# A recurrent memory layer gated by an int-quantised FFN: three elementwise jobs change engine, and the attention jobs move to other slots

## The reference

```
xn = layernorm(x)
# memory: for each of the 2048 steps, M0 is 128 x 128
q, k, v = xn @ Wq.T, xn @ Wk.T, xn @ Wv.T          # 512 -> 128 each
r_t = q_t @ M.T ;  M = 0.99 * M + v_t.T @ k_t / 4
s = (r @ Wo.T) * sigmoid(gate)                     # 128 -> 512
# FFN on layernorm(xn): weights int, one scale for 128 rows of a column
y = silu(h @ dequant(fc1_q) + b1)                  # 512 -> 2048
z = y @ dequant(fc2_q) + b2                        # 2048 -> 512
out = x + s * silu(xn + 0.5 * z)
```

## Time and profile before

| | |
|---|---|
| Time, median of 3 executions | 1356.86 us (1355.76 to 1358.03) |
| The profiled execution's own time | 1356.22 us |
| Its span, first to last instruction | 1354.4 us |
| Share of the span busy: PE, DVE, ACT, POOL | 91%, 80%, 76%, 45% |
| Mean granted TensorE clock | 0.973 |
| DMA engines' mean traffic | 48 GB/s |

### The profile page before, as it was taken

One profiled execution on the slowest core, in us unless ns is written; L12 is line 12 of the kernel. 1 busy time (PEld: TensorE's weight loads), 2 busy tenths in 40 slices (PEclk: granted clock), 3 DMA queues, 4 the chain that ended last, 5 costly groups with the idle time before them and its releaser, 6 DMA issues.

```text
span 1354.4 us, 18593 instructions
## 1 busy us (share of the span) xinstructions
PE 1227.3 (91%) x5888; PEld 588.1 (43%) x5888; DVE 1076.9 (80%) x1829; ACT 1032.3 (76%) x1805; POOL 608.7 (45%) x638
## 2 busy tenths in 40 slices
PE   0359999999999999999999999999999999999993
...
DMA packets 41620, 65.68 MB, mean 48 GB/s; under 512 B 11696, under 2 KB 11952, under 8 KB 41008
## 3 DMA queue, kind: packets, MB, share of 16 engines
...
q10 hardware_dynamic: 288, 0.08, 0.0%
...
## 4 chain that ended last, share of the span: by engine, by line
PE 61%; ACT 22%; issue 10%; DVE 3%; POOL 2%; DMA 1%; SPq 0%; ACTq 0%; POOLq 0%; DVEq 0%
PE blk L447 22%; PE blk L465 20%; PE side L408 9%; ACT blk L550 8%; PE side L432 4%; ACT y_full L557 4%; ACT h_full L512 3%; PE side L424 2%; PE side L417 2%; ACT g_hi L506 2%; ACT y_split L565 2%; ACT z_rows L573 1%; PE side L426 1%; PE side L425 1%; DMA xt<-in_x 1%
## 5 line engine op out<-in xcount | busy, mean ns | idle before, releaser
L680 DVE TENSOR_TENSOR blk<-blk,ratio_rows 128x512 f32<-128x512 f32 x960 | 647.4, 692 | 182.7 <-PE blk L465 180.3
L550 ACT ACTIVATE blk<-blk,ratio 128x512 f32<-128x512 f32 x768 | 519.8, 683 | 181.5 <-PE blk L447 176.1
L447 PE MATMUL blk<-h_split,q_sb 128*128 128x512 f16 x2048 | 614.4, 382 | 43.8 <-ACT q_sb L591 29.0
L465 PE MATMUL blk<-w_sb,y_split 128*128 128x512 f16 x2048 | 609.4, 380 | 6.4 <-POOL w_sb L968 5.6
L465 PEld LDWEIGHTS blk<-w_sb,y_split 128*128 128x128 f16 x2048 | 199.6, 98 | 251.4 <-issue 6.9
L447 PEld LDWEIGHTS blk<-h_split,q_sb 128*128 128x128 f16 x2048 | 183.1, 98 | 289.4 <-ACT blk L550 80.2
L951 POOL TENSOR_TENSOR h_split<-h_full,h_split 128x512 f16<-128x512 f32 x64 | 81.7, 1276 | 478.5 <-DVE h_split L656 464.0
L557 ACT ACTIVATE y_full<-blk,par,last 128x512 f32<-128x512 f32 x256 | 204.6, 799 | 73.5 <-PE blk L447 72.5
L671 DVE SCALAR_TENSOR_TENSOR y_split<-y_full,up,y_split 128x512 f16<-128x512 f32 x256 | 222.5, 869 | 0.0
L565 ACT ACTIVATE y_split<-y_full,up 128x512 f16<-128x512 f32 x256 | 190.7, 745 | 0.0
L999 POOL TENSOR_TENSOR z_rows<-z_rows,s_rows 128x512 f32<-128x512 f32 x62 | 79.0, 1274 | 63.6 <-ACT z_rows L573 63.6
...
## 6 DMA issues: line engine op xcount, KB each, us to landing
...
x_again<-in_x SPq DMA_DIRECT2D x256, 64.0 KB, 1.9
out<-z_rows SPq DMA_DIRECT2D x256, 64.0 KB, 1.7
...
```

Of the source, the lines that this page charges most:

```text
L447: mm = pe.matmul(blk[J % 2][:], q1_sb[:, g, j // 4, w, j % 4 * P:(j % 4 + 1) * P], a[:, c % 2, g, :], start=(g == 0 and n == 0), stop=(g = ...
L465: mm = pe.matmul(blk2[i][:], y[:, J % Y_RING, rows], w2_sb[:, j, part, :], start=(j == 0 and n == 0), stop=(j == FB - 1 and n == len(terms ...
L550: act.activation(blk[J % 2][:], blk[J % 2][:], ACT.Copy, scale=ratio1[:, at:at + 1]).then_inc(blk_scaled, 1)
L680: dve.tensor_tensor(blk2[i][:], blk2[i][:], ratio2_rows[:, j, :], ALU.mult).then_inc(blk2_scaled, 1)
```

## The change

Three jobs change engine: `y_high` goes from ACT to DVE (where `y_low` follows it one slot later, at lag 2 and not 3), and `normalise` and `h_high` go from DVE to POOL. For chunk 0 both stay on DVE, as `first_normalise` and `first_h_high`. The side jobs of a tile stand at offsets 0, 4, 7, 10 and 13 from its start, where they stood at 0, 4, 6, 8 and 11. With tiles 12 slots apart, a tile's wo now comes one slot behind the next tile's qkv. The turns stand at 51, 54, 56 and 59, and their lags are equal for all four. The four PSUM tiles of fc2 become four slices of one tensor; each product still has a bank of its own.

```diff
-TILE_AT, JOB_AT = (1, 13, 25, 37), (0, 4, 6, 8, 11)
-TURN_AT = (49, 52, 55, 58)
-QKV_LAG, QKT_LAG, R_LAG, S_LAG, GHIGH_LAG, HFULL_LAG = 1, 1, 1, 1, 1, (2, 2, 2, 3)
+TILE_AT, JOB_AT = (1, 13, 25, 37), (0, 4, 7, 10, 13)
+TURN_AT = (51, 54, 56, 59)
+QKV_LAG, QKT_LAG, R_LAG, S_LAG, GHIGH_LAG, HFULL_LAG = 1, 1, 1, 1, 1, 2
...
-STATS_AT, MOMENTS_AT, NORMALISE_AT = (0, 1, 2, 3), (5, 6), (33, 34, 37, 40)
-MASK_LAG, MEM_LAG, SPLIT_LAG, YHIGH_LAG, YLOW_LAG = 1, 1, (3, 3, 3, 4), 1, 3
-HLOW_LAG = 5
+STATS_AT, MOMENTS_AT = (0, 1, 2, 3), (5, 6)
+MASK_LAG, MEM_LAG, GLOW_LAG, YHIGH_LAG, YLOW_LAG = 1, 1, 3, 1, 2
+HSPLIT_LAG = 3
+NORMALISE_AT = (36, 38, 40, 42)
...
         @block.scalar
-            def y_high(J):
...
-                act.activation(y_hi[:, J % Y_RING, :], y_full[:, J % 2, :], ACT.Copy, scale=up_y
-                               ).then_inc(y_hi_done, 1)
...
         @block.vector
+            def y_high(J):
+                dve.wait_ge(silu_done, J + 1)
+                wait(dve, blk2_done, NT * (J - Y_RING + 1))
+                dve.tensor_scalar(y_hi[:, J % Y_RING, :], y_full[:, J % 2, :], up_y, None, ALU.mult
+                                  ).then_inc(y_hi_done, 1)
...
         @block.gpsimd
+            def normalise(c, i):
+                if i == 0:
+                    pool.wait_ge(rows_done, c + 1)
+                    pool.wait_ge(turn_done, 4 * c)
+                pool.tensor_scalar(g_rows[:, i, :], xt[:, i, :], mv[:, c % 2, i, 0:1],
+                                   gs[:, c % 2, i:i + 1], ALU.subtract, ALU.mult).then_inc(g_done, 1)
+
+            def h_high(c, k):
+                pool.wait_ge(h_full_done, 4 * c + k + 1)
+                if k == 0 and c >= 2:
+                    pool.wait_ge(blk_done, FC1_COUNT[FB * (c - 1) - 1, KC - 1])
+                pool.tensor_copy(h_hi[:, c % 2, k, :], h_full[:, k % 2, :]).then_inc(h_hi_done, 1)
...
+                if at := job_behind(G, HSPLIT_LAG, "turn"):
+                    h_high(*at)
                     h_low(*at)
```

More of the change, by code:

```diff
@@ L224, in build @@
         blk = [ctx.enter_context(nc.psum_tensor(f"blk{n}", [P, T], F32)) for n in range(2)]
-        blk2 = [ctx.enter_context(nc.psum_tensor(f"blk2_{n}", [P, T], F32)) for n in range(KC)]
+        blk2 = ctx.enter_context(nc.psum_tensor("blk2", [P, NT, H], F32))
         side = [ctx.enter_context(nc.psum_tensor(f"side{n}", [P, T], F32)) for n in range(2)]
-        first_turn_bank = blk2
+        first_turn_bank = [blk2[:, k, :] for k in range(KC)]
         par_in, wq_in, wo_in, m_in, gate_in = (
@@ L464, in ffn2 @@
                 for n, (y, part) in enumerate(terms):
-                    mm = pe.matmul(blk2[i][:], y[:, J % Y_RING, rows], w2_sb[:, j, part, :],
+                    mm = pe.matmul(blk2[:, i, :], y[:, J % Y_RING, rows], w2_sb[:, j, part, :],
                                    start=(j == 0 and n == 0), stop=(j == FB - 1 and n == len(terms) - 1),
@@ L610, in _ @@
                         silu(at[0])
-                if (at := fc1_step(G - YHIGH_LAG) if G >= YHIGH_LAG else None) and at[1] == KC - 1:
-                    y_high(at[0])
                 if at := job_behind(G, QKV_LAG, "qkv"):
@@ L622, in _ @@
                     g_high(*at, side[JOB_BANK[G - GHIGH_LAG]])
-                for k in range(KC):
-                    at = job_behind(G, HFULL_LAG[k], "turn")
-                    if at and at[1] == k:
-                        h_whole(*at, side[JOB_BANK[G - HFULL_LAG[k]]])
+                if at := job_behind(G, HFULL_LAG, "turn"):
+                    h_whole(*at, side[JOB_BANK[G - HFULL_LAG]])
                 if at := finishing(G, GATE_AT):
@@ L638, in moments, with first_h_high, first_normalise @@
                 dve.bn_aggr(mv[:, c % 2, i, :], stat6[:, i, :]).then_inc(mv_done, 1)
-            def normalise(c, i):
+            def first_h_high(k):
+                dve.tensor_copy(h_hi[:, 0, k, :], h_full[:, k % 2, :]).then_inc(first_h_hi_done, 1)
+            def first_normalise(i):
                 if i == 0:
-                    dve.wait_ge(rows_done, c + 1)
-                    wait(dve, turn_done, 4 * c)
-                dve.tensor_scalar(g_rows[:, i, :], xt[:, i, :], mv[:, c % 2, i, 0:1],
-                                  gs[:, c % 2, i:i + 1], ALU.subtract, ALU.mult).then_inc(g_done, 1)
+                    dve.wait_ge(rows_done, 1)
+                dve.tensor_scalar(g_rows[:, i, :], xt[:, i, :], mv[:, 0, i, 0:1],
+                                  gs[:, 0, i:i + 1], ALU.subtract, ALU.mult).then_inc(first_g_done, 1)
             def g_low(c, k, bank):
@@ L650, in g_low @@
                 dve.tensor_tensor(g_lo[:, k, :], bank[:], g_hi[:, k, :], ALU.subtract).then_inc(g_lo_done, 1)
-            def h_high(c, k):
-                if k == 0 and c >= 2:
-                    dve.wait_ge(blk_done, FC1_COUNT[FB * (c - 1) - 1, KC - 1])
-                dve.tensor_copy(h_hi[:, c % 2, k, :], h_full[:, k % 2, :]).then_inc(h_hi_done, 1)
             def mask_scores(c, i, bank):
@@ L794, in _ @@
             for i in range(NT):
-                normalise(0, i)
+                first_normalise(i)
             dve.wait_ge(all_tops_done, 1)
@@ L812, in _ @@
                 g_low(0, n - 1, first_turn_bank[n - 1])
-                h_high(0, n - 1)
+                first_h_high(n - 1)
                 last = top_of_q1(n)
@@ L817, in _ @@
             g_low(0, 3, first_turn_bank[3])
-            h_high(0, 3)
+            first_h_high(3)
             hold(0, s1_c, FB, KC)
@@ L873, in _ @@
                     mask_scores(*at, side[JOB_BANK[G - MASK_LAG]])
-                for k in range(KC):
-                    at = job_behind(G, SPLIT_LAG[k], "turn")
-                    if at and at[1] == k:
-                        g_low(*at, side[JOB_BANK[G - SPLIT_LAG[k]]])
-                        h_high(*at)
+                if at := job_behind(G, GLOW_LAG, "turn"):
+                    g_low(*at, side[JOB_BANK[G - GLOW_LAG]])
                 if at := job_behind(G, MEM_LAG, "read"):
                     remember(*at, side[JOB_BANK[G - MEM_LAG]])
+                if (at := fc1_step(G - YHIGH_LAG) if G >= YHIGH_LAG else None) and at[1] == KC - 1:
+                    y_high(at[0])
                 if (at := fc1_step(G - YLOW_LAG) if G >= YLOW_LAG else None) and at[1] == KC - 1:
@@ L899, in _ @@
                         moments(c + 1, 2 * MOMENTS_AT.index(e) + i)
-                if ahead and e in NORMALISE_AT:
-                    normalise(c + 1, NORMALISE_AT.index(e))
         @block.gpsimd
@@ L1053, in _ @@
                     row_scales(c + 1)
-                if at := job_behind(G, HLOW_LAG, "turn"):
+                if c < NCH - 1 and e in NORMALISE_AT:
+                    normalise(c + 1, NORMALISE_AT.index(e))
+                if at := job_behind(G, HSPLIT_LAG, "turn"):
+                    h_high(*at)
                     h_low(*at)
```

30 lines of the change are left out of this document (17 added, 13 removed).

## The result

| | before | after |
|---|---|---|
| median of 4 runs, us | 1356.34 | 1311.72 |
| lowest to highest, us | 1355.76 to 1358.03 | 1310.97 to 1312.44 |
| span of the profiled execution, us | 1354.4 | 1309.4 |

The ratio is 0.9669, with a 95% interval from 0.9652 to 0.9686: 45 us less, where the prediction had 22 and a range that began at 1312. The direction was right, and so was the stall for DVE's queue. The gain was twice what I had worked out, because waits that I had added to that stall didn't come.

What follows compares the result with a forecast made beforehand. PE's own pace was taken as the bound, 72.7 of 78.50 us a chunk. Stalls of 3.0 + 1.2 = 4.2 for 5.8 save 1.6, 15 times: 1356.2 - 24 + 2 = 1334 us; 8-in-10 range 1312 to 1358.

Steps and rivals of the forecast that it cites:

- The floor and the ceiling: Steady chunk: PE's own work takes 72.7 of 78.50 us, so reordering can win at most 5.8, some 87 us in all.
- PE must stand still for 1.6 us here even if nothing on DVE is ever held up: Slot 52 to the read in slot 11: DVE's queue takes 25.0 us, PE arrives after 23.6.
- 1.4 us on top of the 1.6: Slots 60 to 5: DVE's y operations wait for POOL, two full waits and small ones, 1.4 us a chunk; bounds 0 and 7.4.
- rival A: DVE and POOL miss each other in slots 60 to 5: 3.6 us less a chunk, 1304 us; chance 0.15.
- Rival C: POOL's splits come late and hold up ACT's `h_whole` and `rescale`: 6 to 12 us, 1343 us; chance 0.10.
- y_high is exposed exactly as y_low is: On DVE, `y_high` can be locked out by POOL through shared SBUF ports as `y_low` is; said to speak against the change.
- The rest: 1.2: Slots 12 to 51: PE still loses 1.2 us a chunk: masks 0.6, ACT in slots 16 to 21 0.3, the 0.07s 0.3.
- the 0.07s: Lateness of 0.07 us inside reads and scores, between their matmuls; half left standing, 0.3 us a chunk.
- ACT: Without `y_high`, ACT gains 10 us a chunk and is busy near 52; its lateness of 0.7 lies inside DVE's 1.6.
- POOL's prices: On POOL, a cast was bounded by 0.76 and 1.27 and taken as 0.9 us; `normalise` as 0.76 to 0.87.
- In chunk 0 I give back 2 us: Chunk 0: DVE also makes fc2's high parts and the first tile's waits differ, so 2 us of the gain are lost.

Runs made afterwards that it cites:

- experiment 7: The changed kernel with `normalise` back on DVE, and the mask put ahead of its slot's `block2_out` in DVE's order: 1292.60 us.
- experiment 9: The changed kernel with `normalise` back on DVE, and both the mask and `g_low` ahead of their slot's `block2_out`: 1291.13 us.
- experiment 4: The changed kernel with `h_high`, the cast of h, put back from POOL to DVE: 1352.80 us.
- experiment 8: The changed kernel with `normalise` back on DVE, and `y_high` and `y_low` one slot later each: 1328.04 us.
- experiment 5: The changed kernel with POOL's `normalise` written as multiply then add, plus two small POOL operations a chunk for the new factor: 1316.31 us.
- Experiment 2: The changed kernel with `y_high` put back on ACT and `y_low` at lag 3 again: 1333.62 us.
- experiment 3: The changed kernel with the four `normalise` of a chunk put back on DVE, in slots 36, 38, 40 and 41: 1306.15 us.
- experiment 6: The changed kernel with `normalise` back on DVE, and chunk 0's pieces of fc2's weights two slots later: 1307.24 us.

## Why the prediction was right or wrong

**The floor and the ceiling: right.** PE's 72.7 us a chunk bounded what any reordering could give; experiments 7 and 9 stop 1.3 above it.

**"PE must stand still for 1.6 us here even if nothing on DVE is ever held up": right.** Slots 59, 0, 5 and 11 lose 1.6. Part of it shows before the read, as I had allowed. `y_high`, taken as 0.48 from rows at 0.424 and 0.545, is 0.47 to 0.48. That the queue is the cause, experiments 4, 7 and 9 show: more work ahead of the mask costs in full, one `block2_out` less there (0.60) takes 0.59 from the first read's 0.83, and another order ahead of the mask changes nothing.

**"1.4 us on top of the 1.6": the step that failed.** I laid POOL's splits against DVE's y operations from a chain of estimates (a cast of 0.9 that is 0.61 alone, a `rescale` at 0.57, a slot pace of 77 us), and read two full waits from it. There are none: all of these y operations take their time alone, and the stretch costs 1.6 and not 3.0. In chunks 1 to 14 that is 14 x 1.4, about 20 us, nearly all of the 22 that the forecast missed. My rival A was this case, with its mechanism, and I gave it 0.15. Rival C, ACT held up by POOL's splits, didn't come either: in the steady chunks ACT waits for PE alone. What I should have seen is that the outcome depends on offsets of 0.1 to 0.5 us, and my sum was not that good. Experiments 8 (one slot on DVE) and 4 (another releaser) bring waits of 0.4 to 0.7 us back into the stretch, and experiment 5 (0.6 us of shift on POOL) adds two of 0.6 behind it. Between 0 and 2.4 us both ends were open, and the middle was a choice, not a finding.

**"y_high is exposed exactly as y_low is": right, and it decided nothing in the changed kernel.** At 711.84 `y_high` takes 1.52 and ends 1.54 after POOL's start at 711.82. Less 0.476 of its own, it began its work at 712.88, 0.20 before POOL's recorded end; `y_low` in the earlier trace rows gives the same 0.2. So the wait holds for an operation with one source as well. The Trainium skill (SBUF — State Buffer, Who interferes with whom) says this of a tensor_scalar in a two-port mode, and the trace agrees with the wait; which mode the operation ran in, it doesn't show. What mattered was where the wait falls: 4.0 us a chunk in slots 12 to 37 cost PE at most 0.44, and 2.4 between slots 52 and 11 cost 1.5, although 0.66 of work had gone (experiment 8).

**"The rest: 1.2": twice too much.** The masks of tiles 1 and 2 lose 0.44 (I had 0.6, for waits of this kind), ACT around slot 20 0.16 (0.3), and the 0.07s, left half standing, are within these. Together 0.6, another 0.6 us a chunk.

**ACT: right in kind, undervalued.** I expected ACT busy near 52 and found 55.1; the slack was enough all the same, and PE waits for it 0.32 at slot 0 and 0.16 at slot 20, no more. Experiment 2 shows that the move from ACT carries 22 us by itself, with nothing else changed but the lag of `y_low`, and every stall of PE over 0.1 us in it stands before an fc1 step, which waits for ACT.

**POOL's prices: one nearly right, one wrong.** The cast has a mean of 0.84 (I took 0.9), though alone it takes 0.61, below the bound of 0.76 that I had given it. `normalise` is 2.2 us where I took "0.76 to 0.87, the price of its other tensor_scalar". The row that I took it from multiplies and then adds; this one subtracts and then multiplies. I had bounded an unseen pair of operations by another pair. The order isn't the reason, as POOL's widening L975 adds first and then multiplies, from int32, in 0.69 us. In a steady chunk it costs nothing, since POOL idles there, which experiment 3 shows.

**"In chunk 0 I give back 2 us": mis-sized as well.** Less the 1.6 that I counted as a gain in each of 15 chunks, this made chunk 0 0.4 us longer. It is 7.8 longer. About 4.5 of it is the place of `normalise` (experiment 3). The turn in slot 59 waits 1.7 with `normalise` on either engine, and I had no term for it. The wait at `wo` has grown over the one that stood at fc2: PE comes to slot 17 3.2 later, of which 1.9 is won back by slot 46; experiment 6 moves it back there with no gain in the end.

**The account.** Steady chunks give 3.6 instead of 1.6: 1.4 from the waits that didn't come and 0.6 from the rest. Chunks 1 to 14 give some 28 us more than I had (chunk 1 0.8 more than the steady ones), and the last 105.6 us, where I had put nothing, 2.4. Chunk 0 takes back 7.4 and the start 0.6. 22 + 28 + 2.4 - 7.4 - 0.6 = 44.4 of the 45. The parts don't add up by themselves: undone one at a time they cost 26, 22, 41 and -5.5 us, far more than the 45 together. The first leaves DVE a slot less up to the first read, the next two fill ACT's or DVE's queue in the same stretch, and the third adds waits for POOL that the changed kernel doesn't have there. The turns' new slots, the lags of `h_full` and `g_lo` and the single tensor for fc2's products were never undone alone, so their share is open.
